# Product keys: one head's pair sums on TensorE, two sets of buffers for the other heads' sums, the top-eight search in two halves

## The reference, cut to what matters

```python
def _L1_ffn_ref(x, w_q, keys, expert_down, expert_up, norm_w):   # H = 8 heads, K = 8 kept, NKEYS = 32
    xn = _rmsnorm(x, norm_w)
    q = (xn @ w_q.T).reshape(b, t, H, 2, DK)
    sim1 = jnp.einsum('bthd,hkd->bthk', q[..., 0, :], keys[:, :, 0, :])
    sim2 = jnp.einsum('bthd,hkd->bthk', q[..., 1, :], keys[:, :, 1, :])
    s1, i1 = jax.lax.top_k(sim1, K)
    s2, i2 = jax.lax.top_k(sim2, K)
    all_sc = (s1[..., :, None] + s2[..., None, :]).reshape(b, t, H, K * K)
    fs, pk = jax.lax.top_k(all_sc, K)
    ...                               # fi: expert i1*32 + i2 of each kept pair
    hidden = gelu(xn . expert_down[fi]) * relu(fs)
    return sum of hidden * expert_up[fi]
```

## Time and profile before

| | |
|---|---|
| median of 3 runs | 2663.31 us (2662.86 to 2665.55) |
| the profiled execution | 2666.33 us, span 2664.6 us |
| k5a passes, first weigh of the first tile to that of the last | 445.0 us |
| k7a passes, the same | 441.4 us |
| busy in the whole span | PE 79%, DVE 84%, ACT 70%, POOL 61% |

### The profile page before, as it was taken

How to read it: one execution, slowest core, us unless ns; L and a number is a source line. 1 busy time by engine, 2 the same in 40 slices (tenths; PEclk the granted TensorE clock), 3 DMA queues, 4 the chain that set the end, 5 groups by cost and what they waited for, 6 DMA issues and landing times. The chain is left out here.

```text
span 2664.6 us, 59310 instructions
## 1 busy us (share of the span) xinstructions
PE 2092.7 (79%) x17450; PEld 1738.0 (65%) x17451; DVE 2249.4 (84%) x5529; ACT 1863.0 (70%) x4276; POOL 1620.6 (61%) x1481
## 2 busy tenths in 40 slices
PE   6558888879599999693588877888888448888888
PEld 3246666757588888473466656777777237777777
DVE  7589999865688888657888857999999788999998
ACT  4689999656555555563255548999998349999997
POOL 0079999637200000375566538999999209999997
PEclk9779999989899999797699988999999769999999
DMA  2023333151200000111100000000000000000000
GB/s 49 2 68 95 97 95 100 56 152 51 58 1 0 0 0 1 53 52 38 41 2 0 0 1 1 0 0 0 0 0 0 1 0 1 8 4 4 4 4 8
DMA packets 67622, 69.82 MB, mean 26 GB/s; under 512 B 10248, under 2 KB 46304, under 8 KB 67488
## 3 DMA queue, kind: packets, MB, share of 16 engines
q1 hardware_dynamic: 59408, 56.33, 7.1%
q0 software_dynamic: 4992, 10.23, 1.4%
q10 hardware_dynamic: 3088, 1.62, 0.2%
HBM read 56.50 MB, written 11.67 MB: 26 GB/s over the span
## 5 line engine op out<-in xcount | busy, mean ns | idle before, releaser
L1973 POOL TENSOR_TENSOR k5a_psums<-k5a_sims 128x1024 f32<-128x1024 f32 x224 | 421.6, 1913 | 17.3 <-DVE k5a_w L2181 12.0
L1973 POOL TENSOR_TENSOR k7a_psums<-k7a_sims 128x1024 f32<-128x1024 f32 x224 | 421.7, 1914 | 13.9 <-DVE k7a_w L2181 8.7
L1068 POOL TENSOR_TENSOR mc_hc<-mc_h,mc_cs 128x512 f32<-128x512 f32 x256 | 327.8, 1296 | 32.9 <-DVE mc_h L1035 17.5
L2038 PE MATMUL k5a_pw<-g_ident,k5a_w 128*128 128x128 f32 x2048 | 265.5, 277 | 70.6 <-DVE k5a_hid L2189 45.9
L2038 PE MATMUL k7a_pw<-g_ident,k7a_w 128*128 128x128 f32 x2048 | 262.0, 276 | 70.1 <-DVE k7a_hid L2189 45.9
L2038 PEld LDWEIGHTS k5a_pw<-g_ident,k5a_w 128*128 128x128 f32 x2048 | 226.7, 141 | 113.9 <-DVE k5a_w L2181 52.9
L1035 DVE TENSOR_TENSOR_SCAN mc_h<-mc_dA,mc_inj 128x512 f32<-128x512 f32 x256 | 298.8, 1200 | 2.4 <-PE mc_inj L924 1.8
L2038 PEld LDWEIGHTS k7a_pw<-g_ident,k7a_w 128*128 128x128 f32 x2048 | 227.3, 141 | 109.4 <-issue 63.8
L2181 DVE SCALAR_TENSOR_TENSOR k7a_w<-k7a_psums,k7a_best,k7a_lift 128x1024 f32<-128x1024 f32 x224 | 279.6, 1272 | 0.5 <-ACT k7a_lift L2109 0.3
L2181 DVE SCALAR_TENSOR_TENSOR k5a_w<-k5a_psums,k5a_best,k5a_lift 128x1024 f32<-128x1024 f32 x224 | 279.1, 1270 | 0.5 <-ACT k5a_lift L2109 0.3
L2109 ACT ACTIVATE k7a_lift<-k7a_psums 128x1024 f32<-128x1024 f32 x224 | 229.2, 1023 | 37.6 <-DVE k7a_w L2181 33.2
(11 more groups left out here) (503 smaller groups left out, 5863.2 us busy)
## 6 DMA issues: line engine op xcount, KB each, us to landing
mc_cs<-c_rows SPq DMA_DIRECT2D x128, 256.0 KB, 3.1
e_w<-in_L_ffn_W_dram SPq DMA_DIRECT2D x16, 256.0 KB, 5.5
token_rows<-e_zn SPq DMA_DIRECT2D x16, 256.0 KB, 3.7
e_zn<-token_out SPq DMA_DIRECT2D x16, 256.0 KB, 5.1
out_dram<-g_X SPq DMA_DIRECT2D x7, 256.0 KB, 2.3
e_zs<-token_rows,e_token POOLq DMA_INDIRECT x78, 2.6
token_out<-e_ys,e_token POOLq DMA_INDIRECT x78, 2.3
g_X<-in_L_attn_a_x_dram SPq DMA_DIRECT2D x4, 256.0 KB, 4.7
```

The source lines that it names most:

```text
L1068: nc.gpsimd.tensor_tensor(hc[:, q % RH, :], h_[:, q % RB, :], cs[:, S % RC, :], ALU.mult).then_inc(outs, 1)
L1973: nc.gpsimd.tensor_tensor(psums[:, h - 1, :, :], rows_of(p, h), s2, ALU.add).then_inc(pooled, 1)
L2038: ins = nc.tensor.matmul(pw[:, j, :], w[:, h % WR, j * P:(j + 1) * P], env.ident[:, :], start=(h == 0 and j % 4 == 0), stop=(h == HD - 1 a ...
```

## The change

Head 2's pair sums now come from PE. ACT makes the bf16 high part of that head's 64 scores (`leading`); DVE subtracts it from the scores (`leave`); ACT makes the middle part of the rest (`second`); DVE the low part (`trail`). PE turns the three parts of both sides (`turn`, two matmuls into `pmix`), ACT copies them out (`carry`), and PE multiplies them by a table of ones (`pair`, four matmuls, into a `lift` buffer). ACT copies that sum to `esum` (scaled by 1 + 2^-22), in the place where it took the head's relu. POOL makes no sums for head 2, but 20 of the 32 rows for head 0; ACT makes the other 12. DVE's `form` is gone. `psums` has two sets, so that POOL's `form` waits for the `weigh` two tiles back. `top8` is cut in two: half of it between `weigh(t, 0)` and `finish`, half (and `leave`) between `weigh(t, 1)` and `weigh(t, 2)`. `sim(t + 2)` stands one `sum_up` later and waits for `carry`. POOL builds the table of ones ahead of each stage, from a table that one more DMA on SP's queue loads at the program's start.

The core of the diff:

```diff
-        begin(nc, env, tag + "f", (1.0, 1e-6, 0.0, 1.0), True, ZT, g[:, 0:1], weights, len(weights))
+        begin(nc, env, tag + "f", (1.0, 1e-6, 0.0, 1.0), True, ZT, g[:, 0:1], weights, len(weights), on_pool=place)
...
-            dsum, psums = sb("dsum", [P, K, K]), sb("psums", [P, NP, K, K])
+            psums, esum = sb("psums", [P, 2, NP, K, K]), sb("esum", [P, NE])
+            parts, rest = sb("parts", [P, 2, PARTS, K], BF16), sb("rest", [P, 2, K])
+            simT = sb("simT", [PARTS * K, 2, P], BF16)
...
+                def turn(t):
+
+                    need(pe, low, t + 1)
+                    need(pe, added, t - 1)
+                    for z in range(2):
+                        ins = nc.tensor.matmul(pmix[0:PARTS * K, z * P:(z + 1) * P], parts[:, z, :, :].rearrange("p a k -> p (a k)"),
+                                               env.identb[:, :], start=True, stop=True)
+                    ins.then_inc(split, 1)
+
+                def pair(t):
+
+                    need(pe, entered, t + 1)
+                    need(pe, weighed, t * HD + HP + 1 - LR)
+                    for q in range(2):
+                        for z, e in enumerate((q, 2)):
+                            ins = nc.tensor.matmul(lift[:, HP % LR, q * 512:(q + 1) * 512], simT[:, z, :],
+                                                   ones[:, e, :, :].rearrange("p i j -> p (i j)"), start=(z == 0), stop=(z == 1))
+                    ins.then_inc(paired, 1)
...
+                def carry(t):
+
+                    need(act, split, t + 1)
+                    need(act, paired, t)
+                    nc.scalar.copy(simT[:, :, :].rearrange("p z c -> p (z c)"), pmix[0:PARTS * K, 0:2 * P]).then_inc(entered, 1)
...
+                    if h == HP:
+                        need(act, paired, t + 1)
+                        need(act, weighed, (t - 1) * HD + HP + 1)
+                        nc.scalar.activation(esum[:, :], lift[:, h % LR, :], ACT.Identity, scale=ABOVE).then_inc(lifted, 1)
+                        return
...
+                def leave(t, p):
+
+                    need(dve, high, t + 1)
+                    need(dve, middle, t)
+                    scores = pmix[:, HP * 2 * K:(HP + 1) * 2 * K].rearrange("p (s k) -> p s k", s=2)
+                    nc.vector.tensor_tensor(rest[:, :, :], scores, parts[:, :, 0, :], ALU.subtract).then_inc(left, 1)
+
+                def trail(t):
+
+                    need(dve, middle, t + 1)
+                    need(dve, split, t)
+                    nc.vector.tensor_tensor(parts[:, :, 2, :], rest[:, :, :], parts[:, :, 1, :], ALU.subtract).then_inc(low, 1)
...
```

More of the change, by code:

```diff
@@ L1987, in tile_sums @@
                 def tile_sums(t, p):
+                    form(t, p, 0)
                     form(t, p, 1)
                     cross(t)
-                    for h in range(2, HD):
+                    for h in POOLED[2:]:
                         form(t, p, h)
@@ L2024, in out @@
                     need(pe, mixed, t + 1)
-                    need(pe, dsummed, ahead)
+                    need(pe, left, ahead)
                     need(pe, added, t)
@@ L2046, in body @@
                         begun, final = first and p == 0, last and p == 1
+                        pair(t)
                         sum_up(t, 0)
@@ L2058, in body @@
                         sum_up(t, 5)
+                        if not final:
+                            turn(t + 1)
+                        sum_up(t, 6)
                         if not last:
                             sim(t + 2, p)
-                        sum_up(t, 6)
                         sum_up(t, 7)
@@ L2066, in _ @@
                 hide(0, 1)
+                turn(0)
                 sim(1, 1)
@@ L2134, in body @@
                             sums(t + 1, 1 - p, 3)
-                        raise_(t, 6)
-                        raise_(t, 7)
+                        raise_(t, p, 6)
+                        raise_(t, p, 7)
                         if not final:
+                            carry(t + 1)
                             gate(t + 1, 1 - p, 1)
@@ L2142, in _ @@
                 enter(0, 0)
+                leading(0, 0)
+                second(0)
                 for q in range(GROUPS):
@@ L2146, in _ @@
                 gate(0, 0, 1)
+                carry(0)
                 rounds(act, NT // 2, body)
@@ L2150, in _, with top8 @@
             def _(dve):
-                def top8(t, p):
-                    need(dve, crossed, t)
-                    hold(dve, s_in, t + 1)
-                    for h in range(HD):
+                def top8(t, p, half):
+                    if half == 0:
+                        need(dve, crossed, t)
+                        hold(dve, s_in, t + 1)
+                    for h in range(half * HD // 2, (half + 1) * HD // 2):
                         for s in range(2):
                             ins = nc.vector.max(top[:, h, s, :], sims[:, p, h, s, :])
-                    ins.then_inc(topped, 1)
+                    if half:
+                        ins.then_inc(topped, 1)
                 def rank(t, p):
@@ L2180, in weigh @@
                     need(dve, lifted, t * HD + h + 1)
[L2181 removed]
+                    nc.vector.scalar_tensor_tensor(w[:, h % WR, :], sums_of(p, h), best[:, p, h, 7:8], lift[:, h % LR, :],
                                                    ALU.is_ge, ALU.mult).then_inc(weighed, 1)
@@ L2201, in _ @@
                 dve.wait_ge(floored, 1)
-                top8(0, 0)
-                form(0, 0)
+                top8(0, 0, 0)
+                top8(0, 0, 1)
+                leave(0, 0)
+                trail(0)
                 rank(0, 0)
@@ L2210, in body @@
                         weigh(t, p, 0)
+                        if not final:
+                            top8(t + 1, 1 - p, 0)
                         if not begun:
@@ L2214, in body @@
                         if not final:
-                            top8(t + 1, 1 - p)
+                            top8(t + 1, 1 - p, 1)
+                            leave(t + 1, 1 - p)
                         weigh(t, p, 2)
-                        if not final:
-                            form(t + 1, 1 - p)
                         weigh(t, p, 3)
@@ L2222, in body @@
                             rank(t + 1, 1 - p)
+                            trail(t + 1)
                         weigh(t, p, 5)
```

86 lines of the change are left out of this document (53 added, 33 removed).

## The result

| | before | changed |
|---|---|---|
| median on the same chip | 2664.43 us (2662.86 to 2670.97, 4 runs) | 2715.50 us (2713.71 to 2719.21, 4 runs) |
| profiled execution | 2666.33 us | 2713.71 us, span 2711.7 |
| k5a, first weigh of the first tile to that of the last | 445.0 us | 466.1 us |
| k7a, the same | 441.4 us | 466.1 us |
| steady tile, k5a and k7a | 14.40, 14.28 us | 14.83, 14.83 us |

The ratio is 1.0183, 95% interval 1.0171 to 1.0196: slower by 51 us, where 37 were forecast (2701 us). The forecast tile was 14.90 us.

The account below looks back on a forecast made before the run. It took a loop between PE and DVE, 14.28 us per tile, to bound the kernel. The new loop's 14.90 us per tile and 2.8 us of stage starts added 38.0 us to 2666.33; forecast 2701 us, range 2686 to 2771.

Parts of the forecast that it names:

- The loop: From weigh 2's end through PE's `sum_up` 5, `turn`, `carry`, `gate`, `raise_`, then DVE to weigh 2: 14.90 us per tile.
- The sizes: Times put on the loop's new parts: `turn` 0.28 us, handover to ACT 0.06, `carry` 0.25, `leave` 0.16.
- The first passes: Each stage's first pass, without `finish`, was put at 13.8 us.
- the port: DVE's `trail`, both inputs in SBUF, waits a whole POOL form: 1.1 us more per tile, 2770 us; chance 0.17.
- the likeliest case: The forecast itself, 14.90 us per tile and 2701 us, with 2688 to 2746 from its bounds; chance 0.66.
- The stage's start: Ahead of each stage's first pass ACT waits for the search and `leave`: 1.4 us with `carry`, twice, 2.8 in all.
- What stood at nothing: `pair` (1.1 us inside PE's 1.49 us wait), `esum`, later `sim`, ACT's sums and casts, POOL's work: no added time.

Follow-up runs that it names:

- e2: The changed kernel with `turn` moved on PE ahead of head 5's `sum_up`; 2686.00 us, ratio 1.0067 to the kernel before.
- e7: The changed kernel with `trail` on POOL, `turn` ahead of `sum_up` 5 and `sim` right behind that `sum_up`; 2648.57 us, ratio 0.9932 to the kernel before.
- e3: The changed kernel with `trail` moved from DVE to POOL, behind `cross`; 2703.45 us, ratio 1.0135 to the kernel before.
- e1: The changed kernel with `carry` moved on ACT behind the second `gate` and the next tile's first `raise_`; 2712.34 us, ratio 1.0172 to the kernel before.
- e9: The changed kernel with `trail` ahead of `rank` on DVE, 0.79 us earlier; 2726.14 us, ratio 1.0221 to the kernel before.
- e5: The changed kernel with an empty POOL instruction behind each `form` in the written-out passes; 2716.67 us, ratio 1.0193 to the kernel before.
- e4: The changed kernel with the search in one piece again, behind weigh 1; 2702.59 us, ratio 1.0133 to the kernel before.

## Why the prediction was right

- *The loop.* Forecast from rows of before: 14.90 us per tile through `turn`, `carry`, `gate`, `raise_` and both halves of the search, in both stages. Measured 14.83 in both, each link in the trace, weigh 0 waiting 1.32 us in k7a's tile above where 1.3 was worked out (0.79 at the median in k5a, where `statistics` lie in that wait, as forecast). That moving `turn` (e2, e7) took time off the tile shows that this loop set it; e7's 13.95 is the sum of the same terms, with `turn` earlier.
- *The sizes.* `carry` 0.27 to the next start (0.25 taken), `turn` 0.11 on PE and 0.31 to `carry`'s start (0.28 + 0.06), `leave` 0.12 (0.16), the two other handovers 0.03 (0.06). They make up the 0.07 us.
- *Where it fell short.* The first passes: 13.8 forecast, 21.13 measured, 7.3 us twice. 6.7 of each comes from `trail`'s wait for POOL's run of forms, as e3 shows by taking it away: 5.3 us in k7a and 5.6 in k5a are the wait itself; of the rest most is a longer wait in front of weigh 0 (in k7a 1.68 us for 0.71 in e3), behind PE's slow `sum_up` 5. The other 0.6 stays in e3 (14.38), where the first half of the search waits 0.58 us for `enter`. The rival "the port" had the mechanism right, and for the steady tile the phase too (`trail` comes 0.15 to 0.23 us ahead of a form's end, 0.1 to 0.3 forecast); what it missed is that a wait can last over more than one form, as it does in the first pass. The forecast's sum had no term for it. That the time lies even within the likeliest case's 2688 to 2746 is due to the width of that range and not to its reasons.
- *The stage's start.* 1.4 us each was forecast; from the first `bring` to the first weigh 0 it is 12.77 us where it was 12.34, so 0.4. The terms are there: ACT's sums begin 2.0 us later behind `enter` and take 2.65 us for 3.50. But the first `sim` took 1.12 us where it took 2.08, which no term had: in k7a PE's granted clock was 1.00 around it (the level of 2.4 GHz), before the change 0.50 (1.2 GHz), though PE had idled 1.52 us ahead of it in both.
- The sum: 38.0 forecast between the profiled executions; 2 x 7.3 for the first passes, less 2 x 2.0 for the shorter tiles and 2 x 1.0 for the starts, makes 46.6; measured 2713.71 - 2666.33 = 47.4. By parts, 30.0 us come from the 60 steady passes, 15.8 from the two first passes (21.13 for 13.22) and 0.9 from the two starts.
- *What stood at nothing.* `pair`, `esum` and POOL's work were covered in the steady tile, as forecast. `sim` one head later was put down as out of the loop; it was, by 0.58 us. The expectations for e1 and e2 overlooked that loop, which in both sets the tile.

## What to carry to other kernels

When one engine's in-order program gets a new wait, look at what stands behind it: here a 0.27 us copy held up a `raise_` that the busiest engine waits for. A wait that disappears (in front of `finish`) says nothing of the period; go around the loop and see whether the moved work is still in it, and how far the next loop is behind, since that one takes over where the first is cut: here one of 14.25 us behind one of 14.83 (e2). A move can also lengthen the next loop, as e1's did. With five steps moved (`trail` to POOL; `turn`, `sim`, `hide` and `out` earlier on PE) the same change is worth 1.4% instead of costing 1.8%.

## What was not expected of the hardware

A DVE subtraction of 64 columns with both inputs in SBUF and the result in bf16 takes 0.21 us, and up to 6.63 us while POOL works back to back. In the loops it always got in at the end of the running form (56 executions of e9: 1.01 to 1.10 us, with 0.93 to 1.02 to that end). The Trainium skill, "SBUF — State Buffer", section "SBUF: two separate sides", says that the one that comes second is blocked for the other's whole instruction; e9's loops agree. In the first passes it often did not get in between two forms and waited for the rest of the run, two or three forms more than the one that ran. Each of these waits ended with the last form: `trail` itself ended 0.08 to 0.09 us behind it.

The phase doesn't decide it: 0.14 to 0.17 us ahead of a form's end, `trail` was 0.23 us long in the loop and 5.85 in k5a's first pass. Nor does an instruction between the forms, as the loop has, decide it alone: with an empty one k7a's first pass waited as long (e5), and in the second pass, whose forms are written out without one, it got in after a single form (0.89 us in e9). One thing goes with it in every run that has `trail` on DVE: the nine long ones (5.48 to 6.63 us) all come behind a `cross` that followed POOL's forms without a wait, so that POOL was behind its work. Where `cross` had waited, if only 0.20 us as in e4's first passes, none waited for more than one form. The one short `trail` behind a `cross` without a wait is k5a's in e5 (0.24 us), with the empty instruction. No run was made to separate POOL's lateness from what goes with it, so the cause stays open.
